# Row scales of a quantised feed-forward part found for two row tiles at a time instead of one

## What is computed

```
def _fake_quant_lastdim(x):
    s = jnp.max(jnp.abs(x), axis=-1, keepdims=True) / QMAX      # one scale per row
    s = jnp.maximum(s, 1e-08)
    return jnp.clip(jnp.round(x / s), -QMAX, QMAX) * s

def _dyn_quant_linear(x, w, b):
    return jnp.einsum('bti,oi->bto', _fake_quant_lastdim(x), _fake_quant_lastdim(w)) + b

h = _layernorm(vit_embeds, gamma, beta)
h = _dyn_quant_linear(h, w1, b1)
h = jax.nn.gelu(h, approximate=False)
h = _dyn_quant_linear(h, w3, b3)
x = x + h
```

## Time and profile before

| | us |
|---|---|
| median of 3 runs (1591.23 to 1593.21) | 1591.58 |
| the profiled execution's own time | 1589.58 |
| its span in the profile | 1587.8 |
| PE busy in the span | 1494.7 |
| DVE busy in the span | 957.3 |
| last DVE instruction of the program ends at | 1585.2 |

### The profile page before, as it was taken

How to read it: one execution, slowest core, us unless ns; L and a number is a source line. 1 busy time by engine, 2 the same in 40 slices (tenths; PEclk the granted TensorE clock), 3 DMA queues, 4 the chain that set the end, 5 groups by cost and what they waited for, 6 DMA issues and landing times. The chain is left out here.

```text
span 1587.8 us, 28705 instructions
## 1 busy us (share of the span) xinstructions
PE 1494.7 (94%) x11536; PEld 1281.4 (81%) x11536; DVE 957.3 (60%) x1954; ACT 588.2 (37%) x1416; POOL 569.6 (36%) x468
## 2 busy tenths in 40 slices
PE   4999999999999978998679999999999999999986
PEld 3788888888888867886569888888999888889973
DVE  6666566665666665664846545565555546555587
ACT  3222132222222215442235444443544444344456
POOL 2544363443535304662223222231222223141248
PEclk8999999999999998999879999999999999999998
DMA  6111020111102002220211101010111101010201
GB/s 177 40 41 41 28 63 25 48 34 34 53 16 67 1 21 60 79 55 0 71 50 34 35 28 41 14 55 2 41 28 28 41 28 41 1 54 16 72 10 53
DMA packets 81229, 64.44 MB, mean 41 GB/s; under 512 B 7280, under 2 KB 66928, under 8 KB 81104
## 3 DMA queue, kind: packets, MB, share of 16 engines
q1 hardware_dynamic: 80240, 62.47, 13.6%
q10 hardware_dynamic: 864, 0.20, 0.1%
HBM read 60.56 MB, written 2.10 MB: 39 GB/s over the span
## 5 line engine op out<-in xcount | busy, mean ns | idle before, releaser
L142 POOL TENSOR_TENSOR att_w_lo<-att_w_raw,att_w_hi 128x512 fp32r<-128x512 f32 x160 | 202.8, 1293 | 174.4 <-ACT att_w_hi L137 174.4
L1294 POOL TENSOR_TENSOR att_probs<-att_probs,att_total 128x512 f32<-128x512 f32 x64 | 82.8, 1294 | 476.7 <-DVE att_total L1033 357.6
L70 PE MATMUL att_proj<-att_w_hi,kv_hi 128*128 128x256 f32 x768 | 223.5, 291 | 8.6 <-PEq L223 8.6
L70 PE MATMUL att_proj<-att_w_lo,kv_hi 128*128 128x256 f32 x768 | 218.7, 285 | 0.0
L70 PE MATMUL att_proj<-att_w_hi,kv_lo 128*128 128x256 f32 x768 | 218.6, 285 | 0.0
L70 PE MATMUL att_proj<-att_w_hi,att_o_hi 128*128 128x512 f32 x512 | 206.0, 402 | 6.0 <-issue 3.9
L70 PE MATMUL att_proj<-kv_hi,att_w_hi 128*128 128x512 f32 x512 | 207.2, 405 | 0.0
L70 PE MATMUL att_proj<-kv_lo,att_w_hi 128*128 128x512 f32 x512 | 201.9, 394 | 0.0
L70 PE MATMUL att_proj<-kv_hi,att_w_lo 128*128 128x512 f32 x512 | 201.4, 393 | 0.0
L70 PE MATMUL att_proj<-att_w_lo,att_o_hi 128*128 128x512 f32 x512 | 200.9, 392 | 0.0
L70 PE MATMUL att_proj<-att_w_hi,att_o_lo 128*128 128x512 f32 x512 | 200.8, 392 | 0.0
(11 more groups left out here) (152 smaller groups left out, 2945.1 us busy)
## 6 DMA issues: line engine op xcount, KB each, us to landing
att_w_raw<-in_wq SPq DMA_DIRECT2D x64, 256.0 KB, 2.9
att_w_raw<-in_wo SPq DMA_DIRECT2D x64, 256.0 KB, 2.7
ln_stage<-in_ctx_t SPq DMA_DIRECT2D x8, 512.0 KB, 5.0
att_w_raw<-in_wk SPq DMA_DIRECT2D x16, 256.0 KB, 3.0
att_w_raw<-in_wv SPq DMA_DIRECT2D x16, 256.0 KB, 3.2
ffn_w_raw<-in_gate_t SPq DMA_DIRECT2D x10, 256.0 KB, 2.9
ffn_w_raw<-in_up_t SPq DMA_DIRECT2D x10, 256.0 KB, 3.1
ffn_w_raw<-in_down_t SPq DMA_DIRECT2D x10, 256.0 KB, 3.0
```

What stands on the lines that cost most here:

```text
L70: ins = eng.matmul(out, a, b, start=(first and n == 0), stop=(last and n == 3 * len(terms) - 1))
L142: eng.tensor_tensor(self.lo[:, chunk], self.raw[:, n % RAW_SLOTS], raw(self.hi[:, chunk]), ALU.subtract)\
L1294: eng.tensor_tensor(probs[:, u % 2, 0:n], probs[:, u % 2, 0:n], total[:, u % 2, 0:n].unsqueeze(2).broadcast_to([P, n, KL]), ALU.mult)\
```

## The change

`find_scale` becomes `find_scales`, which takes `count` items, two unless told otherwise. It takes the magnitudes of both items one after the other (in items 4 to 7 each behind its `beta` addition), and then one instruction finds both scales and one both reciprocals; the latter raises `inverted` by two. Items 0 and 1 keep a call each; items 2 and 3 share one. In the loop from item 4 on, a pass now handles two items: the scales of items n and n+1, and then the two products n-2 and n-1 are scaled one after the other. What PE, ACT, POOL and SP carry out, and in which order, stays as it is.

```
-    def find_scale(self, eng, chain, n):
-        l, t = self.ITEMS[n]
...
-        one = slice(n, n + 1)
-        chain.step(eng.tensor_reduce(self.top[:, one], self.y[:, t], AX.X, ALU.max, apply_absolute_value=True))
-        chain.step(eng.tensor_scalar(self.scale[:, one], self.top[:, one], 1.0 / QMAX, 1e-8, ALU.mult, ALU.max))
-        eng.reciprocal(self.inv[:, one], self.scale[:, one]).then_inc(self.inverted, 1)
+    def find_scales(self, eng, chain, n, count=2):
+        for i in range(n, n + count):
+            l, t = self.ITEMS[i]
...
+            ins = eng.tensor_reduce(self.top[:, i:i + 1], self.y[:, t], AX.X, ALU.max, apply_absolute_value=True)
+        chain.step(ins)
+        some = slice(n, n + count)
+        chain.step(eng.tensor_scalar(self.scale[:, some], self.top[:, some], 1.0 / QMAX, 1e-8, ALU.mult, ALU.max))
+        eng.reciprocal(self.inv[:, some], self.scale[:, some]).then_inc(self.inverted, count)
...
-            tail.find_scale(eng, chain, 2)
-            tail.find_scale(eng, chain, 3)
+            tail.find_scales(eng, chain, 2)
             tail.dequant(eng, 0)
             tail.dequant(eng, 1)
             tail.copy_weight_row(eng, 1)
-            for n in range(4, len(tail.ITEMS) + 2):
+            for n in range(4, len(tail.ITEMS) + 2, 2):
                 if n < len(tail.ITEMS):
-                    tail.find_scale(eng, chain, n)
-                tail.dequant(eng, n - 2)
-                if n - 2 in tail.LATE:
-                    tail.finish(eng, n - 2)
+                    tail.find_scales(eng, chain, n)
+                for i in (n - 2, n - 1):
+                    tail.dequant(eng, i)
+                    if i in tail.LATE:
+                        tail.finish(eng, i)
```

More of the change, by code:

```diff
@@ L480, in base @@
         eng.tensor_tensor(self.st.x[:, t], self.st.x[:, t], self.rows["b3"][:], ALU.add).then_inc(self.based, 1)
-    def find_scale(self, eng, chain, n):
-        l, t = self.ITEMS[n]
[L484 to L492, removed]
-        one = slice(n, n + 1)
-        chain.step(eng.tensor_reduce(self.top[:, one], self.y[:, t], AX.X, ALU.max, apply_absolute_value=True))
-        chain.step(eng.tensor_scalar(self.scale[:, one], self.top[:, one], 1.0 / QMAX, 1e-8, ALU.mult, ALU.max))
-        eng.reciprocal(self.inv[:, one], self.scale[:, one]).then_inc(self.inverted, 1)
+    def find_scales(self, eng, chain, n, count=2):
+        for i in range(n, n + count):
+            l, t = self.ITEMS[i]
+            if l == 0 and t < 4:
+                eng.wait_ge(self.offset, t + 1)
+            elif l == 0:
+                eng.wait_ge(self.weighted, t + 1)
+                if t == 4:
+                    eng.wait_ge(self.rows_landed, 64)
+                chain.step(eng.tensor_tensor(self.y[:, t], self.y[:, t], self.rows["beta"][:], ALU.add))
+            else:
+                eng.wait_ge(self.gelued, t + 1)
+            ins = eng.tensor_reduce(self.top[:, i:i + 1], self.y[:, t], AX.X, ALU.max, apply_absolute_value=True)
[3 more added lines that the diff above has]
+        eng.reciprocal(self.inv[:, some], self.scale[:, some]).then_inc(self.inverted, count)
     def round(self, eng, n):
@@ L1117, in _ @@
             tail.copy_weight_row(eng, 0)
-            tail.find_scale(eng, chain, 0)
+            tail.find_scales(eng, chain, 0, 1)
             add_out(g, 1, 0)
             add_out(g, 1, 1)
-            tail.find_scale(eng, chain, 1)
+            tail.find_scales(eng, chain, 1, 1)
             add_out(g, 1, 2)
```

## The result

| | us |
|---|---|
| median before, 22 runs (1588.44 to 1593.58) | 1591.29 |
| median after, 22 runs (1591.89 to 1600.43) | 1594.62 |
| ratio after / before, 95% interval | 1.0022 [1.0014, 1.0029] |
| profiled execution of after: own time, span | 1594.47, 1592.7 |

The medians differ by 3.3 us; the ratio gives 0.22%, 2.2 to 4.6 us by its interval. The forecast was 1594.0, or +2.4. Its sum is short by about one microsecond, and that microsecond can be found row by row.

What follows compares the result with a forecast made beforehand. A loop of waits among PE, DVE and ACT, no engine full, was taken to bound the last 40 us. Start +0.79, loop +1.80 and end -0.16 sum to +2.43; on the median 1591.58 that gives 1594.0 us, range 1591.9 to 1596.7.

Steps and rivals of the forecast that it cites:

- the likeliest case's own range: Whole time if the sum holds as worked out, chance 0.52: 1593.3 to 1594.8 us, or +1.7 to +3.2.
- The loop: Items 8 to 14: a pair's turn through PE, DVE and ACT grows from 4.10 to 4.70 us; three turns cost +1.8.
- Another 0.60: On DVE in each turn: the magnitude of item b, new ahead of the shared scale and reciprocal, adds 0.60 us.
- A wider scale (two columns for one) I price as the old one: On DVE: the scale instruction for two items was taken to last as long as for one, 0.16 us.
- The start: Items 2 to 8, ahead of the loop: item 8's rounding comes at 1566.6 instead of 1565.82, costing +0.8 us.
- the walk: Prediction's instruction-by-instruction timing of items 2 to 8, putting item 4's rounding at 1555.32, item 6's at 1561.84, item 8's at 1566.6.
- The end: From item 14's rounding: item 15's follows after 1.97 us instead of 2.13, giving back 0.16; the list after stays.
- The clock falls on the path: Rival, chance 0.38: PE drops to 1.2 GHz after idle holes; one low turn gives +3.7 us, two give +5.0.
- DVE is the limit and the pairing saves: Rival, chance 0.03: DVE never waits for products, so seven pairs save 0.38 us each, 2.7 us, giving 1588.9.
- hidden anyway: Rival, chance 0.07: DVE would wait for b's product anyway, hiding b's magnitude; time stays at 1591.6 to 1592.4 us.
- the signs named ahead: Expected in the profile after: two magnitudes in a row, roundings 4.70 apart, DVE waits of about 1.7 us, DVE's end near 1587.6.
- Within 0.2%: Whole time changes by no more than 3.2 us, not to be told from none: chance 0.58, against 0.40 for slower.

Runs made afterwards that it cites:

- the first experiment: Kernel before with only the changed kernel's DVE order, each item keeping its own scale and reciprocal: 1589.58 us, ratio 0.9996 [0.9987, 1.0004].

## Why the prediction was right, and by how much it was off

The measured 1594.62 lies in the likeliest case's own range, 1593.3 to 1594.8. No large errors cancelled in it: all but the end came out dearer than forecast. The baseline helped a little, as the median before is now 1591.29 and not 1591.58.

- **The loop.** Right in place and kind. "Another 0.60" ahead of scale and reciprocal: the chain shows 1.20 for two magnitudes, the new order with separate reciprocals stays at 4.10, a spare magnitude in the old kernel gives 4.69 to 4.70, and the changed kernel with the semaphore raised by one gives 4.70 in the one turn that has next to no hold. Taking product b-2 out from behind a's transposes takes DVE off the chain and brings the turn to 4.11, so both halves of the loop are shown; in the whole time only part of the loss came back with it (ratio 1.0014).
- **"A wider scale (two columns for one) I price as the old one"** is the step that was mis-sized. The seven scales took 0.17 to 0.99, the three ahead of items 10, 12 and 14 0.30, 0.31 and 0.17. The separate wait of 0.07 a turn was not in the sum at all. With both, the three turns come out at +2.31 and not +1.80: two holds of 0.15 over the old scale, and three times 0.07. The prediction let the additions of beta wait for POOL and did not ask whether the scale would wait too when its shape changed.
- **The start**, +0.79 forecast, was +1.37. Counted from magnitude 2, the rounding of item 4 came 0.26 later than in the walk, that of item 6 0.55 and that of item 8 0.59. The first two steps are the scales at 0.39 and the separate waits: 0.39 - 0.16 + 0.07 = 0.30 each. The waits named in the walk for additions of beta behind POOL were there. The longest hold, 0.99 ahead of items 2 and 3, cost nothing: it went into the wait of the addition for item 4, which took 0.85 and not 1.40 and ended 5.28 after magnitude 2 in both kernels.
- **The end**: -0.16 forecast, -0.18 measured.
- **The clock falls on the path** (0.38): not in the profiled execution, where transposes take 0.66 from item 4 on. The holes were there, 1.78, 1.51 and 2.26 us before the transposes of items 4, 5 and 6, where the prediction estimated 1.5 to 1.9 each; the clock held behind the 2.26 too. The low stretch that before had on the path at item 5 is missing. The walk counted on that, with product 4 off the path behind the additions of beta; the first experiment bears it out. What a low clock can do once turns get longer was seen with the product between the magnitudes, and with PE in pairs (items 5 to 7). The changed kernel's times spread over 8.5 us where those of before spread over 5.1; low turns in some executions would fit that, but there is no profile of a slow one, so it is only argued.
- **DVE is the limit and the pairing saves** (0.03) and **hidden anyway** (0.07): no. DVE waited 10.6 us for products, and the chain runs from the scaling into both magnitudes without a gap. A turn shorter than that of before came only when PE and ACT worked in pairs as well, and POOL was the next limit then.
- Of the signs named ahead: two magnitudes in a row, waits before every second scaling of 1.68 to 1.69 us, as said. Distances of 4.70 were 4.91, 4.92 and 4.77; item 8's rounding at 1566.6 was at 1568.58 and the last DVE instruction's end, near 1587.6, at 1590.11, of which 1.39 each is the later start of the tail.
- "Within 0.2%" had the larger chance, 0.58; the ratio, 1.0022, lies just beyond, and its interval has both in it. So whether the change is slower by over 0.2% stays undecided; that it is slower is clear.

**Open.** Which tensor's place makes the difference in the second attention, and by what mechanism, is not known: no run moved `att_o` alone. The tails of the two new-order kernels are 1.7 to 2.5 us below those of their partners, of which their medians show nothing certain. And in all six profiles with a shared reciprocal the second attention's first matmul starts at 806.2 to 807.4, in the three of the same layout without it at 804.2 to 804.9. Each is one execution, and kernels with the column, alike up to there, differ as much (804.4 to 808.8). The medians' interval, 2.2 to 4.6 us, has the tail's 3.50 in it and not the 4.89 of the profiled executions; that the change costs nothing ahead of the tail is likely by this, but not shown.

## What to carry to other kernels

Where engines wait for each other in turn, write down one turn of the loop before grouping anything: an instruction taken away off the loop gave nothing here, and a shared result makes the first consumer wait for the last producer. In this kernel grouping on DVE alone lost 0.22%; with its partners' lists grouped alike the loss was gone, but no gain over before showed in the time. After changing the shape of a tiny instruction look at its minimum and maximum, not only its mean; and when an edit also allocates something, run the allocation alone.

## What the runs showed of the hardware

- A `tensor_scalar` on 128x2 fp32 was held until the POOL instruction under way was done: it lasted 0.17 to 1.19 us. On 128x1 it took 0.15 in all 14 cases, beside the same kind of POOL work. A reciprocal on 128x2 was not held (0.165 to 0.167).
- With the reciprocal raising its semaphore by two, the wait ahead of it stood in the trace as an entry of its own and cost about 0.07 us; raised by one, it did not.
- One unused column in SBUF made three forms of 128x512 matmul go from 394 to 396 ns to 389 and the program 0.31% faster, more than the whole change under study costs. All five kernels with the column have 389, and all nine without it 394 to 396.
- An addition with both inputs in SBUF on DVE took 0.69 us with POOL between two instructions and 4.09 beside five POOL additions in a row (products scaled three behind): it ended 0.56 after the last of them.
